# Linear attention's keys' and values' products: one head per 64 by 64 tile on the array's column halves, four pairs of heads to a bank, in place of one pair per 128 by 128 block

## The reference, cut to what matters

```python
Q = sigmoid((x @ W_Q).reshape(B, N, 16, 64))
K = sigmoid((x @ W_K).reshape(B, N, 16, 64))
V = (x @ W_V).reshape(B, N, 16, 64)
KV = einsum('bnhk,bnhv->bhkv', K, V)          # one 64 x 64 matrix for each of 16 heads
num = einsum('bnhk,bhkv->bnhv', Q, KV)
den = einsum('bnhk,bhk->bnh', Q, K.sum(axis=1))[..., None] + 1e-8
x = (num / den).reshape(B, N, 1024) @ W_fc + x
```

## Time and profile before

| | |
|---|---|
| median of 3 runs | 1052.21 us (1050.7 to 1052.64) |
| time of the profiled execution | 1050.82 us |
| its span (first to last instruction) | 1049.0 us |
| mean granted clock of TensorE | 0.993 |
| PE busy | 1014.6 us, 97% |
| DVE busy | 374.3 us, 36% |
| ACT busy | 204.0 us, 19% |
| POOL busy | 318.2 us, 30% |

### The profile page before, as it was taken

How to read it: one execution, slowest core, us unless ns; L and a number is a source line. 1 busy time by engine, 2 the same in 40 slices (tenths; PEclk the granted TensorE clock), 3 DMA queues, 4 the chain that set the end, 5 groups by cost and what they waited for, 6 DMA issues and landing times.

```text
span 1049.0 us, 10308 instructions
## 1 busy us (share of the span) xinstructions
PE 1014.6 (97%) x3530; PEld 541.9 (52%) x3530; DVE 374.3 (36%) x1055; ACT 204.0 (19%) x418; POOL 318.2 (30%) x246
## 2 busy tenths in 40 slices
PE   6999999999999999999999999999999999998987
PEld 4555555555555545544555565544444455445422
DVE  6034472056100057811154101163102167586314
ACT  3123221111111027810021112011011010002400
POOL 2787887878888820000001000010000000000310
PEclk9999999999999999999998999999999999999999
DMA  9655545544544551012075888771532115644996
GB/s 331 184 100 141 140 101 140 133 108 99 130 106 105 134 180 41 2 60 101 21 245 190 315 318 336 272 268 62 192 107 97 63 41 194 248 128 180 401 367 248
DMA packets 63709, 173.81 MB, mean 166 GB/s; under 512 B 22208, under 2 KB 22944, under 8 KB 63536
## 3 DMA queue, kind: packets, MB, share of 16 engines
q1 hardware_dynamic: 38800, 146.56, 40.8%
q0 software_dynamic: 20816, 15.10, 8.1%
q10 hardware_dynamic: 4048, 11.59, 3.1%
HBM read 161.27 MB, written 11.95 MB: 165 GB/s over the span
## 4 chain that ended last, share of the span: by engine, by line
PE 87%; DMA 6%; DVE 3%; issue 2%; ACT 2%; SPq 0%; ACTq 0%; DVEq 0%; POOL 0%; POOLq 0%
PE bank L1039 36%; PE bank L1050 16%; PE bank L1026 9%; PE bank L1275 7%; PE bank L1300 3%; PE bank L1474 3%; PE bank L1589 2%; DMA rows<-in_stream 2%; PE bank L1140 2%; PE bank L1431 1%; DMA Y<-in_stream 1%; PE bank L1608 1%; DMA Y<-xs,idx 1%; PE bank L1126 1%; PE bank L1259 1%
## 5 line engine op out<-in xcount | busy, mean ns | idle before, releaser
L1039 PE MATMUL bank<-xnT,ring 128*128 128x384 f32 x896 | 292.4, 487 | 1.7 <-ACT xnT L706 1.1
L1039 PEld LDWEIGHTS bank<-xnT,ring 128*128 128x128 f32 x896 | 169.6, 190 | 122.3 <-issue 3.6
L539 POOL DMA_INDIRECT n_lo<-count,ridx x48 | 83.2, 1734 | 15.5 <-issue 14.0
L539 POOL DMA_INDIRECT n_hi<-count,ridx x48 | 81.7, 1702 | 18.7 <-issue 13.1
L593 POOL DMA_INDIRECT Y<-xs,idx x9 | 8.7, 966 | 256.7 <-DMA xs<-xn 178.4
L1050 PE MATMUL bank<-ring,Y 128*128 128x512 f32 x192 | 83.9, 595 | 0.0
L1050 PE MATMUL bank<-ring,xnT 128*128 128x512 f32 x192 | 82.7, 592 | 0.0
L1039 PE MATMUL bank<-Y,ring 128*128 x256 | 82.7, 486 | 0.0
L593 POOL DMA_INDIRECT G<-xs,idx x2 | 2.2, 1124 | 256.0 <-DVE idx L2254 248.2
L1275 PE MATMUL bank<-ring,Y 128*128 128x352 f32 x256 | 77.2, 460 | 0.0
L730 ACT ACTIVATE Y<-bank,sbias,scale 128x384 f32 (+1 forms) x48 | 32.2, 671 | 202.3 <-PE bank L1039 175.4
(11 more groups left out here) (339 smaller groups left out, 1144.3 us busy)
## 6 DMA issues: line engine op xcount, KB each, us to landing
ring<-in_stream SPq DMA_DIRECT2D x144, 512.0 KB
ring<-in_up SPq DMA_DIRECT2D x32, 704.0 KB, 5.5
Y<-in_stream SPq DMA_DIRECT2D x18, 512.0 KB, 5.8
G<-in_stream SPq DMA_DIRECT2D x16, 512.0 KB, 6.3
ring<-in_dn SPq DMA_DIRECT2D x7, 1024.0 KB, 5.6
rows<-keys SPq DMA_DIRECT2D x10, 512.0 KB
ys<-Y ACTq DMA_DIRECT2D x9, 512.0 KB, 7.0
xnT<-in_stream SPq DMA_DIRECT2D x6, 512.0 KB, 11.6
```

What stands on the lines that cost most here:

```text
L539: pool.indirect_dma_start(table, bass.IndirectOffsetOnAxis(ap=at[:, e:e + 1], axis=0), what[:, e:e + 1], None, **how).then_inc(done, 16)
L1039: last = pe.matmul(bank[to][:, 0:N], ring[:, r, k * P:(k + 1) * P], rhs(k), start=(k == 0), stop=(k == KB - 1))
```

## The change

K and V are multiplied by head. `V1` is laid out by head: 64 columns of V and one of ones. For head `h` of pair `a` the stationary block is the head's 64 columns of K, and the result, 64 by 65, goes to partitions `h * 64` on, columns `a % 4 * 65` on, of bank 0 for the first four pairs and bank 1 for the last four. The products of different heads are no longer computed, so no mask is needed. DVE takes four pairs at once: a copy of 4 by 64 columns into `kv` and a multiplication of ones by the sums into `ks`, and both pieces stand before the minimum of `elu` and no longer behind it. PE waits for a bank only before the Q chunk that writes to it: the first chunk for bank 0, the second for bank 1. `PR_NUM`, the count at which the taking of pairs starts, goes from 14 to 8, and with it the waits of SP that name it; `attend` reads the new tiles with the same four products.

```diff
-PR_NUM = PR_KV + 8
+PR_NUM = PR_KV + 2
...
-        V1 = G[:, 4608:4608 + NB * 1040].rearrange("p (b a c) -> p b a c", b=NB, a=8)
+        kv = G[:, 0:512].rearrange("p (a c) -> p a c", a=8)
+        ks = G[:, 7776:8288].rearrange("p (a c) -> p a c", a=8)
+        V1 = G[:, 4608:4608 + NB * 1040].rearrange("p (b h c) -> p b h c", b=NB, h=HEADS)
...
-            for a in range(8):
-                if a == 0:
+            for g in range(2):
+                if g == 0:
                     pe.wait_ge(product_taken, 1)
-                if a >= 2:
-                    pe.wait_ge(product_taken, PR_KV + a - 1)
-                for b in range(NB):
-                    last = pe.matmul(bank[a % 2][:, 0:130], K[:, b, a * P:(a + 1) * P], V1[:, b, a, :],
-                                     start=(b == 0), stop=(b == NB - 1))
+                for a in range(4 * g, 4 * g + 4):
+                    c = slice(a % 4 * (DH + 1), (a % 4 + 1) * (DH + 1))
+                    for b in range(NB):
+                        for h in range(2):
+                            last = pe.matmul(bank[g][h * DH:(h + 1) * DH, c], K[:, b, a * P + h * DH:a * P + (h + 1) * DH],
+                                             V1[:, b, 2 * a + h, :], start=(b == 0), stop=(b == NB - 1),
+                                             skip_group_check=True)
                 last.then_inc(product_ready, 1)
...
             for m in range(KB):
-                if m == 0:
-                    pe.wait_ge(product_taken, PR_NUM)
+                if m < 2:
+                    pe.wait_ge(product_taken, PR_KV + m + 1)
                 chunk_T(m, lambda k: xnT[:, k, :], T_Q + m - 1, arr(3)(m), m % 2)
...
+            for g in range(2):
+                v.wait_ge(product_ready, PR_KV + g + 1)
+                sums_ = bank[g][:, 0:4 * (DH + 1)].rearrange("p (a c) -> p a c", a=4)
+                v.tensor_copy(kv[:, 4 * g:4 * g + 4], sums_[:, :, 0:DH])
+                tt(ks[:, 4 * g:4 * g + 4], ones[:, 0:DH].unsqueeze(1).to_broadcast([P, 4, DH]),
+                   sums_[:, :, DH:DH + 1].to_broadcast([P, 4, DH]), ALU.mult).then_inc(product_taken, 1)
             v.wait_ge(product_taken, PR_KV)
             ts(Y[:, 5, :], Y[:, 4, :], 0.0, None, ALU.min).then_inc(act_input, 1)
-            for a in range(8):
-                v.wait_ge(product_ready, PR_KV + a + 1)
-                tt(kvbd[:, a, :], bank[a % 2][:, 0:P], bd, ALU.mult)
-                ts(ksbd[:, a, :], ones, bank[a % 2][:, P:P + 1], None, ALU.mult).then_inc(product_taken, 1)
             v.wait_ge(act_output, EL)
```

More of the change, by code:

```diff
@@ L357, in program @@
         A16 = w[:, 800:812].bitcast(F16).rearrange("p (b e) -> p b e", b=NB)
-        kvbd = G[:, 0:1024].rearrange("p (a c) -> p a c", a=8)
-        ksbd = G[:, 7776:8800].rearrange("p (a c) -> p a c", a=8)
-        V1 = G[:, 4608:4608 + NB * 1040].rearrange("p (b a c) -> p b a c", b=NB, a=8)
+        kv = G[:, 0:512].rearrange("p (a c) -> p a c", a=8)
+        ks = G[:, 7776:8288].rearrange("p (a c) -> p a c", a=8)
+        V1 = G[:, 4608:4608 + NB * 1040].rearrange("p (b h c) -> p b h c", b=NB, h=HEADS)
         CET = G[:, 1040:1040 + NB * N].rearrange("p (b n) -> p b n", b=NB)
@@ L961, in _ @@
                 for b in range(NB):
-                    act.activation(V1[:, b, 4 * half:4 * half + 4, 0:P],
-                                   bank[2 + 3 * half + b][:].rearrange("p (a c) -> p a c", a=4),
+                    act.activation(V1[:, b, 8 * half:8 * half + 8, 0:DH],
+                                   bank[2 + 3 * half + b][:].rearrange("p (h c) -> p h c", h=8),
                                    ACT.Copy).then_inc(hkv_done, 1)
@@ L1452, in attend @@
                 lower, upper = slice(0, DH), slice(DH, P)
-                for to, what, own, other in ((4 + 2 * (a % 2), kvbd, lower, lower), (4 + 2 * (a % 2), kvbd, upper, upper),
-                                             (5 + 2 * (a % 2), ksbd, lower, upper), (5 + 2 * (a % 2), ksbd, upper, lower)):
-                    last = pe.matmul(bank[to][other, 0:N], what[own, a, other], YT(1)[own, a, :], start=True, stop=True,
+                for to, what, own, other in ((4 + 2 * (a % 2), kv, lower, lower), (4 + 2 * (a % 2), kv, upper, upper),
+                                             (5 + 2 * (a % 2), ks, lower, upper), (5 + 2 * (a % 2), ks, upper, lower)):
+                    last = pe.matmul(bank[to][other, 0:N], what[own, a, :], YT(1)[own, a, :], start=True, stop=True,
                                      skip_group_check=True)
@@ L2187, in _ @@
             step(last)
-            v.memset(V1[:, :, :, P:P + 2], 1.0)
+            v.memset(V1[:, :, :, DH:DH + 1], 1.0)
             v.wait_ge(product_ready, 1)
```

## The result

Over 11 executions the changed kernel takes 1048.26 us (1044.8 to 1049.33), the kernel before 1052.35 us (1050.64 to 1053.95): ratio 0.996, interval 0.995 to 0.997. It is faster by 4.1 us, with 3.2 to 5.3 us inside the interval, where 5.6 had been summed. The profiled execution took 1046.18 us with a span of 1044.3 us, against 1050.82 and 1049.0.

A forecast was written before the change was run, and what follows sets the result against it. PE was taken to bound the kernel, with 87% of the chain; shorter matmuls and removed waits for DVE bring Q from 851.45 to 845.9, 5.6 us less, so 1052.21 becomes 1046.6, stated as 1046.5 us, range 1044.0 to 1050.2.

The forecast's parts named there:

- Matmuls and issue: Keys' and values' products on PE: 48 side-by-side pairs of 54 ns take 2.6 us, with a start every 27 ns.
- Changes of the array's shape: PE around the heads' products: switching from full array to halves costs 0.15 us, and back 0.10 us.
- DVE: Taking of bank 0: begins at 844.7, ends at 845.5, 0.4 us before the first Q chunk needs it at 845.9.
- The minimum behind: DVE's minimum after the takings: first attend round 1.2 us late, caught up by the second pair; no cost on the path.
- Series or added cost: Rival at the heads' products: halves do not overlap or each matmul costs extra; gain 3.0 us, time 1049.2; chance 0.11.
- Weight loads not hidden: Rival at the heads' products: loads cannot lie under the previous matmul; slower, 1053.3 to 1057 us; chance 0.05.
- Given back by DMA: Rival from 965 us on: the full DMA queue's start does not move, all 5.6 us lost, time 1052.2; chance 0.11.
- The 0.5 us of cover ahead of 909.1: Output projection's fourth slot: all eight pairs ready at 908.56, PE arrives at 909.1; both ends expected to shift together.
- The sum: Q projection starts at 845.9 against 851.45, so the whole kernel takes 5.6 us less.
- Everything from 900 on 5.6 us earlier: Sign to look for in the stages behind: all shifts 5.6 us earlier with PE, the last stage's loads too.

The follow-up runs named there:

- e2: Changed kernel with the lower heads of four pairs first, then the upper, so the two halves do not alternate; ratio 0.9976 to before, median 1049.14 us.
- e1: Changed kernel with DVE's minimum of elu put back ahead of the two takings; ratio 0.9971 to before, 3.1 us below it.
- e12: Kernel before with 16 idle matmuls put ahead of the first Q chunk, so Q starts later; ratio 1.0039, 4.1 us above before.
- e9: Changed kernel with 12 idle matmuls ahead of the first Q chunk, giving back part of the gain; ratio 0.9964 to before, median 1049.34 us.
- e6: Changed kernel with four more idle matmuls ahead of the third block's transposes in the features stage; ratio 0.996 to before, median 1047.47 us.
- e10: Changed kernel with six more idle matmuls in the features stage, four ahead of the third block's transposes, two around its affinities; ratio 0.9934, median 1046.23 us.
- e8: Changed kernel with 33 idle matmuls between the heads' products and the first Q chunk, so Q starts where it did before; ratio 1.0015 to before.
- e3: Kernel before with only the minimum of elu moved behind its eight takings; ratio 1.0003 to before, 0.3 us above it.

## Why the prediction was right, and where it was off

*Matmuls and issue.* 54 ns for a round of two was said, and 27 ns for each start as just possible; 29 were measured. In series it is 53 (e2). The sum 2.6 us became 2.8. Right, 0.2 us too good.

*Changes of the array's shape.* 0.15 in and 0.10 out were summed. In: 841.40 against the slot at 841.31, 0.09. Out: the last of 96 starts at 844.20 and Q at 844.35, 0.15 in place of 0.03 for a bare step, so 0.12. Right together.

*DVE.* The copy of 256 was taken as 0.425 and is 0.43; the multiplication, taken as 0.42 between two bounds, is 0.41. DVE was done 0.5 us before Q started. Right, and e1 shows what the cover is worth: without the new order it is overdrawn by 0.35 us.

*The minimum behind.* The first round of `attend` on DVE should have been 1.2 us late and caught up by the second. It began at 857.01, 2.1 us behind its matmuls where before it was 1.0, so 1.1 us late, and the second waited for PE again, 0.66 us. Nobody on the path noticed. Right.

*The rivals.* Series or added cost: out by e2 against the changed kernel. Weight loads not hidden: out by the same 29 ns. Given back by DMA: out in the last stage, which takes 84.1 us against 83.8 before. The 0.5 us of cover ahead of 909.1 did not turn into a wait: from the first Q chunk to the output projection it is 48.95 us in both kernels, and PE does not wait in the projection.

*The sum, and the term that was off.* "Everything from 900 on 5.6 us earlier" is where it was off. At 900 the stretch had given 5.4 (measured in every profile of the changed kernel); the median gave 4.1. The prediction took the stages behind as a rigid block that shifts with PE. In all three profiles of the changed kernel the features stage is 1.9 to 2.1 us longer, at 1.2 GHz for 10.2 us. The trace of before could not show that: the stage is at full clock there. It did show that the clock falls at all, at 544 to 562 in the first layer's routing and again near 1020, and that PE has little and small work in the features stage while DVE sets the pace. I had checked that stage for waits and transfers, not for its clock. e12 shows that shifting the stage, by idle work that changes nothing in it, is enough to lose the clock, and e9's profile that it can keep it with an early Q. In e6's profile a little more work on PE shortens the drop, in e10's it is gone. The number of 1046.5 us was 1.8 too low, within the range.

How much of the shortfall is the drop's is argued, not shown. The three measurements of the changed kernel give 4.1, 4.3 and 5.4 us; 5.6 is inside the interval of the second and the third, and the third has the drop in its profile like the others. With the drop away e10 gives 5.6 to 8.4 us, and e6, with most of it away, no more than the changed kernel.

What stays open: why the place of the drop repeats so well from one execution to the next, and what that place is counted from. All three profiles of the changed kernel have it and both of before do not, though PE reaches L1431 at times 2 us apart in them. Every profile also has half-clock stretches in the first layer's routing, around 543 to 564 us, and those may tie what follows to them; that is argued, not shown. Nor is it shown in what share of the timed executions the drop falls. That e8 is above before is open too.

## What to carry to other kernels

Products of 64 by 64 on the diagonal of a 128 by 128 block are worth cutting by head when the halves can alternate: half the columns, no mask, and more results to a bank, which took PE's waits for the evictions away. Of the 5.5 us of the stretch the reordering on VectorE would have given 1.8 by itself, and the rest needed the banks and the halves. A shorter stretch is not yet a shorter program: with the reordering alone (e3) the time did not move.

Where a gain of a few microseconds shifts a later stage in which TensorE has only small matmuls, read the granted clock of that stage before and after, and test a missing microsecond by shifting the stage with idle work ahead of it. A few idle matmuls within such a stage may be worth more than they take: with six more the drop was gone from the profile (e10) and the median 1.2 us lower, which its interval does not yet tell from nothing. Look at the timed runs as well as the profile; with four (e6) only the profile improved.

## What was not expected of the hardware

A drop to 1.2 GHz came in a stage where PE had waited no longer than 0.76 us at a time and was otherwise issuing 8-column matmuls, transposes and six idle matmuls; the same instructions, with the same waits ahead, kept 2.4 GHz in before and in e9 (64.8 us for the stage, 66.9 in the changed kernel). Two halves take turns at 29 ns for a matmul with its weight load, over 96 in a row.
